# Causal attention inside a fused block: diagonal pieces weighed in float32, probabilities kept in a ring of four where the activations X lay

## What is computed

```python
q, k, v = jnp.split(x @ W_qkv, 3, axis=-1)          # 16 heads of 64
q, k = (apply_rope(q), apply_rope(k))
dots = jnp.einsum('bhid,bhjd->bhij', q, k) * scale
dots = jnp.where(causal, neg, dots)
attn = jax.nn.softmax(dots, axis=-1)
out = jnp.einsum('bhij,bhjd->bhid', attn, v)
out = jax.nn.relu(out @ W_o1) @ W_o2                # then layer norm, times gamma
```

## Time and profile before

| | us |
|---|---|
| median of three runs | 5071.18 |
| the profiled execution, its time | 5068.41 |
| the profiled execution, its span | 5066.7 |
| PE busy | 3697.3 (73%) |
| DVE busy | 3704.5 (73%) |
| ACT busy | 2570.4 (51%) |
| POOL busy | 2389.1 (47%) |
| float16 weighing, three lines | 464.4 + 462.7 + 463.2 |
| the 16 turns of attention, from and to | about 2712 to 4565 |

### The profile page before, as it was taken

How to read it: one execution, slowest core, us unless ns; L and a number is a source line. 1 busy time by engine, 2 the same in 40 slices (tenths; PEclk the granted TensorE clock), 3 DMA queues, 4 the chain that set the end, 5 groups by cost and what they waited for, 6 DMA issues and landing times. The chain is left out here.

```text
span 5066.7 us, 84689 instructions
## 1 busy us (share of the span) xinstructions
PE 3697.3 (73%) x28907; PEld 2605.5 (51%) x28907; DVE 3704.5 (73%) x4463; ACT 2570.4 (51%) x4134; POOL 2389.1 (47%) x1532
## 2 busy tenths in 40 slices
PE   2997645555555569948936998999989898994595
PEld 1663224444434446637813665666656565663484
DVE  6993579999999989930067888888888888885101
ACT  1222456666666632222214676777767676784221
POOL 0220268888888832220034666656656666600202
PEclk9998767777777789959958999999999999996697
DMA  2000001001101000024532222222222222202254
GB/s 86 0 0 4 7 21 32 30 29 30 31 29 29 30 28 0 0 96 153 162 118 55 55 54 48 47 49 68 52 64 53 52 53 54 52 10 91 73 181 155
DMA packets 236314, 276.23 MB, mean 55 GB/s; under 512 B 63820, under 2 KB 183557, under 8 KB 234561
## 3 DMA queue, kind: packets, MB, share of 16 engines
q1 hardware_dynamic: 223056, 244.85, 17.8%
q0 software_dynamic: 8704, 24.35, 1.4%
q10 hardware_dynamic: 4224, 2.76, 0.2%
HBM read 152.60 MB, written 36.04 MB: 37 GB/s over the span
## 5 line engine op out<-in xcount | busy, mean ns | idle before, releaser
L2247 DVE TENSOR_TENSOR att_b_prob_low<-att_b_prob,att_b_prob_high 128x1024 f16<-128x1024 f32 (+2 forms) x640 | 780.4, 1220 | 64.0 <-ACT att_b_prob_high L2214 55.2
L2274 DVE TENSOR_REDUCE att_b_neg_max<-att_b_peek 128x1 f32<-128x1024 f32 (+1 forms) x748 | 667.8, 906 | 143.1 <-PE att_b_peek L2102 115.8
L2212 ACT ACTIVATE att_b_prob<-att_b_score,att_soft 128x1024 f32<-128x1024 f32 (+2 forms) x640 | 633.7, 990 | 219.9 <-PE att_b_score L2125 145.7
L1030 PE MATMUL mix_scan_hT<-ident,mix_scan_h 128*128 128x128 f32 x1024 | 248.7, 389 | 536.1 <-DVE mix_scan_h L978 502.1
L2214 ACT ACTIVATE att_b_prob_high<-att_b_score,att_soft 128x1024 f16<-128x1024 f32 (+2 forms) x640 | 630.8, 986 | 10.1 <-PE att_b_o L2153 3.6
L1030 PEld LDWEIGHTS mix_scan_hT<-ident,mix_scan_h 128*128 128x128 f32 x1024 | 172.5, 197 | 650.7 <-DVE mix_scan_h L978 443.9
L2149 PE MATMUL att_b_o<-att_b_vh,att_b_prob_high 128*128 128x65 f16 x4352 | 464.4, 195 | 36.9 <-DVE att_b_prob_low L2247 27.5
L2123 PE MATMUL att_b_score<-att_b_q_both,att_b_k_twice 128*128 128x512 f16 (+3 forms) x1280 | 450.5, 352 | 31.4 <-ACT att_b_prob_high L2214 21.9
L2149 PEld LDWEIGHTS att_b_o<-att_b_vh,att_b_prob_high 128*128 128x128 f16 x4352 | 402.4, 98 | 128.8 <-DVE att_b_prob_low L2247 73.5
L2153 PE MATMUL att_b_o<-att_b_vh,att_b_prob_low 128*128 128x65 f16 x4352 | 463.2, 194 | 0.0
L2151 PE MATMUL att_b_o<-att_b_vl,att_b_prob_high 128*128 128x64 f16 x4352 | 462.7, 193 | 0.0
(11 more groups left out here) (344 smaller groups left out, 9612.7 us busy)
## 6 DMA issues: line engine op xcount, KB each, us to landing
moe_w<-in_L_ffn_W_dram SPq DMA_DIRECT2D x64, 1024.0 KB, 8.1
mix_scan_b_row<-mix_b_rows SPq DMA_DIRECT2D x128, 256.0 KB, 3.2
att_b_crossed<-att_b_raw SPq DMA_DIRECT2D x512, 64.0 KB, 2.0
att_b_q_both<-att_b_halves SPq DMA_DIRECT2D x240, 64.0 KB, 2.0
att_b_k_twice<-att_b_halves SPq DMA_DIRECT2D x240, 64.0 KB, 2.0
moe_slots_in<-moe_route_zero SPq DMA_DIRECT2D x2, 4096.0 KB, 14.6
moe_exp_x<-moe_slots_in SPq DMA_DIRECT2D x32, 256.0 KB, 4.5
moe_slots_out<-moe_exp_y POOLq DMA_DIRECT2D x32, 256.0 KB, 6.5
```

The source lines that it names most:

```text
L1030: last = pe.transpose(hT_ps[:, j * D + m * P:j * D + (m + 1) * P], hs[:, b * W + m * GRP + t * P:b * W + m * GRP + (t + 1) * P], ident[:, :])
L2212: act.activation(prob[:, at:at + width], score[m % 2][:, 0:width], ACT.Exp, scale=soft[:, 0:1])
L2247: dve.tensor_tensor(prob_low[:, at:at + width], prob[:, at:at + width], prob_high[:, at:at + width], ALU.subtract).then_inc(low_ready, 1)
L2274: last = dve.tensor_reduce(neg_max[:, first + col:first + col + 1], peek_bank(kind, s)[:, base:base + nb * P], AX.X, ALU.max, negate=True)
```

## The change

Pieces with the diagonal (WHOLE) are no longer split. ACT writes their exponential once, to float32; DVE does nothing for them; PE weighs each block with one float32 matmul of the float32 probabilities and a float32 copy of V (`v_whole`, 65 columns with its column of ones). For this ACT copies each of V's four jobs twice, to float32 and to float16, the float32 copy first. The other pieces are weighed as before.

`prob` now holds four pieces, and together with `headsT` lies in the first 5120 columns of X. These columns (128 x 5120 float32, 2.5 MB) are stored to `lent` in DRAM when the stage begins, ahead of the tables, and fetched back at the start of the first `attention_out`, behind the fetch of the first sequence's sums; DVE waits for both fetches before it adds to X. ACT waits for the store before the first exponential. The float32 exponential of piece m now waits for the last reader of piece m - 4, which is PE for a diagonal piece and DVE for another. `low_ready` counts split pieces only (`split`).

```diff
+WHOLE = [PIECES_S[n][1][0][0] >= PIECES_S[n][0] * GT for n in range(NH)]
+SPLITS = [m for m in range(STEPS) if not WHOLE[m % NH]]
...
+PROBS = 4
+BORROWED = PROBS * SPAN + 2 * GRP
...
+        v = sb("v", [P, 2 * QT * 2 * COL])
+        v_whole = v[:, :].rearrange("p (s e) -> p s e", e=COL)
-        prob = sb("prob", [P, 2 * SPAN])
+        prob, headsT = X[:, 0:PROBS * SPAN], X[:, PROBS * SPAN:BORROWED]
...
                     load_weights(0, 0)
+                    sp.dma_start(lent, X[:, 0:BORROWED]).then_inc(x_lent, 16)
                     sp.dma_start(cos[:, :], rope[0]).then_inc(tables, 16)
                     sp.dma_start(sin[:, :], rope[1]).then_inc(tables, 16)
...
+            pool.memset(v_whole[:, :, ONE:ONE + 1], 1.0).then_inc(masks, 1)
...
-                pe.wait_ge(low_ready, piece(t, m + 1))
+                if WHOLE[n]:
+                    pe.wait_ge(expd, piece(t, m + 1))
+                else:
+                    pe.wait_ge(low_ready, split(t, m + 1))
...
+                    if WHOLE[n]:
+                        last = pe.matmul(out, prob[:, whole], v_whole[:, s, 0:HEAD + 1], start=first, stop=final,
+                                         skip_group_check=True)
+                        continue
...
+                if kind == FIRST:
+                    act.wait_ge(x_lent, 16)
...
+                    act.copy(v_whole[:, at:at + GT * 2, 0:HEAD], side_ps[:, :].rearrange("p (s d) -> p s d", d=HEAD))
                     act.copy(v_cols[:, at:at + GT * 2, 0:HEAD], side_ps[:, :].rearrange("p (s d) -> p s d", d=HEAD))\
                         .then_inc(v_high, 1)
...
             def exponents(t, m):
-                at, width = m % 2 * SPAN, width_of(m)
+                to, at, width = m % PROBS * SPAN, m % 2 * SPAN, width_of(m)
                 act.wait_ge(scored, piece(t, m + 1))
-                wait_unless_first(act, low_ready, piece(t, m - 1))
-                act.activation(prob[:, at:at + width], score[m % 2][:, 0:width], ACT.Exp, scale=soft[:, 0:1])
+                if WHOLE[(m - PROBS) % NH]:
+                    wait_unless_first(act, p_done, piece(t, m - PROBS + 1))
+                else:
+                    wait_unless_first(act, low_ready, split(t, m - PROBS + 1))
+                ins = act.activation(prob[:, to:to + width], score[m % 2][:, 0:width], ACT.Exp, scale=soft[:, 0:1])
+                if WHOLE[m % NH]:
+                    ins.then_inc(expd, 1)
+                    return
...
-                    if has_piece(kind, v - 1):
+                    if has_piece(kind, v - 1) and not WHOLE[(v - 1) % NH]:
                         low_part(t, v - 1)
...
-            if fetch:
-                sp.dma_start(fetch[0][:, :], fetch[1]).then_inc(fetch[2], 16)
+            for to, parked in fetch:
+                sp.dma_start(to, parked).then_inc(fetched, 16)
...
             steps = QT // GT
+            dve.wait_ge(fetched, 2 * 16)
```

More of the change, by code:

```diff
@@ L1520, in experts_and_attention, with attention_outputs @@
             acc = inner.enter_context(nc.sbuf_tensor(f"{name}_acc", [P, QT * D], F32))
-            attention_heads(nc, ident, dram, rope, xh, xl, unit, per_unit, soft, acc, x_parked, acc_parked, name + "_b")
-            attention_outputs(nc, X, ident, dram, acc, acc_parked, name)
-def attention_outputs(nc, X, ident, dram, acc, acc_parked, name):
+            lent = nc.dram_tensor(f"{name}_lent", (P, BORROWED), F32, kind="Internal").ap()
+            attention_heads(nc, X, ident, dram, rope, xh, xl, unit, per_unit, soft, acc, x_parked, acc_parked, lent,
+                            name + "_b")
+            attention_outputs(nc, X, ident, dram, acc, acc_parked, lent, name)
+def attention_outputs(nc, X, ident, dram, acc, acc_parked, lent, name):
     with ExitStack() as ctx:
@@ L1529, in attention_outputs @@
         fetched = nc.alloc_semaphore(name=f"{name}_fetched")
-        attention_out(nc, X, ident, dram, acc, 1, f"{name}_out1", (earlier, acc_parked, fetched))
-        attention_out(nc, X, ident, dram, earlier, 0, f"{name}_out0", None, fetched)
+        attention_out(nc, X, ident, dram, acc, 1, f"{name}_out1", ((earlier[:, :], acc_parked), (X[:, 0:BORROWED], lent)), fetched)
+        attention_out(nc, X, ident, dram, earlier, 0, f"{name}_out0", (), fetched)
 def combine_for_attention(nc, X, ident, dram, xh, xl, unit, per_unit, soft, x_parked, wide, weight, get, slots_out, name):
@@ L1826, in attention_heads @@
         inv = sb("inv", [P, GT])
-        heads, headsT = sb("heads", [P, QT * PAIR]), sb("headsT", [P, 2 * GRP])
+        heads = sb("heads", [P, QT * PAIR])
         score = [ps("score0", SPAN), ps("score1", SPAN)]
@@ L1850, in attention_heads, with split @@
         piece = lambda t, m: t * STEPS + m
+        def split(t, m):
+            return t * len(SPLITS) + sum(1 for u in SPLITS if u < m) - sum(1 for u in SPLITS if u >= m + STEPS)
         slot = lambda p, s: p * STEPS + s
@@ L2144, in weigh @@
                 for k, at, i in blocks:
+                    whole = slice(m % PROBS * SPAN + at, m % PROBS * SPAN + at + P)
                     at = slice(m % 2 * SPAN + at, m % 2 * SPAN + at + P)
@@ L2246, in low_part @@
                 wait_unless_first(dve, p_done, piece(t, m - 1))
-                dve.tensor_tensor(prob_low[:, at:at + width], prob[:, at:at + width], prob_high[:, at:at + width],
+                dve.tensor_tensor(prob_low[:, at:at + width], prob[:, fro:fro + width], prob_high[:, at:at + width],
                                   ALU.subtract).then_inc(low_ready, 1)
@@ L2313, in _, with attention_out @@
             dve.wait_ge(added, out_count(STREAM, 0))
-def attention_out(nc, X, ident, dram, acc, batch, name, fetch=None, fetched=None):
+def attention_out(nc, X, ident, dram, acc, batch, name, fetch, fetched):
     T0 = batch * QT
@@ L2340, in _ @@
                 .then_inc(w_loaded, 16)
-            if fetch:
-                sp.dma_start(fetch[0][:, :], fetch[1]).then_inc(fetch[2], 16)
+            for to, parked in fetch:
+                sp.dma_start(to, parked).then_inc(fetched, 16)
         @block.scalar
         def _(act):
-            if fetched is not None:
-                act.wait_ge(fetched, 16)
+            if not fetch:
+                act.wait_ge(fetched, 2 * 16)
             def first(t, b):
```

12 lines of the change are left out of this document (6 added, 6 removed).

## The result

The changed kernel takes 5085.6 us (median of 6 runs, 5075.4 to 5091.9), the kernel before 5073.8 on the same chip (6 runs, 5064.5 to 5079.4): ratio 1.0024, 95% interval 1.0014 to 1.0034. It is **slower by 12 us**, where 5035 and a gain were forecast. The profiled execution took 5085.0 us, with a span of 5083.4.

The account below looks back on a forecast made before the run. POOL's chain was taken to bound steps 0 to 22 of a turn, PE and DVE alternately steps 22 to 39. -2.5 us over 15 turns (-37.5) plus +3 at the start, on 5068.4, gave 5034, forecast as 5035 us, range 4980 to 5105.

Parts of the forecast that it names:

- A float32 block costs 0.222: PE's weighing: two records of 0.111 us a block, 0.132 more than before; eighty blocks a turn add 10.6 us.
- rival (c): PE's float32 weighing: load and matmul in series, 0.153 us a record, +5.5 us a turn, 5154 us; chance 0.09.
- POOL's chain loses 3.9 us, the first part 3.5 and 0.5 for the clock: Steps 0 to 22: fewer subtractions shorten POOL's six jobs by 3.9; 0.4 given back for PE; -0.5 for a shorter stall.
- Second part: PE +23 blocks, 3.0 us, where it has 44.3 of work in 48.7 ... I take +1.5: Steps 22 to 39: PE's dearer weighing partly fits in its room; net +1.5 us a turn, ends -1 and +5.
- DVE's relief in the second part: Steps 22 to 39: DVE's 6 us less help only where DVE leads; included in the +1.5 a turn.
- The extra V copies: ACT's float32 copy of V delays PE's next V job by up to 0.59 us, four times a turn.
- ACT's relief costs or gives nothing: Each turn: ACT's 10.4 us net saving is worth nothing by itself, as ACT mostly waits for PE or POOL.
- Start +3 (0 to 12): Before attention: X's store ahead of the tables delays them some 8 to 10 us, just reaching DVE's first rotation; +3 us.
- X's way back: nothing: First attention_out: X is back near 4589, wanted at 4600.8, so no cost; without that cover up to 12 us.
- The last turn: nothing: Last turn, led by ACT: its pairs lose 1.6 us there and gain 1.3 on PE; net nothing.
- rival (b): Each turn: gains and losses cancel, 1.5 in the first part, 1.3 back in the second; 5068 us; chance 0.15.
- rival (a): Steps 22 to 39 and heavy first-part pairs: PE becomes the bound, +3.5 us a turn, 5124 us; chance 0.15.

Follow-up runs that it names:

- e4: Changed kernel, diagonal pieces weighed in float32, but ACT still writes their high part and DVE still subtracts, into unread buffers; ratio 1.0106 to the kernel before.
- e9: Changed kernel with float32 weighing only for head 1's diagonal pieces (steps 20 to 39), head 0 weighed as before; ratio 1.0068 to the kernel before.
- e3: Changed kernel, diagonal pieces without float32 exponential or subtraction, weighed by three float16 matmuls, the third reading the high part; ratio 0.9920 to the kernel before.
- e8: Kernel before, with DVE's instruction in diagonal pieces reading scores from PSUM instead of float32 probabilities from SBUF; PE's scores wait for it; ratio 0.9967.
- e1: Changed kernel with only the ring of four and X's store and fetch kept, all pieces weighed as before, no float32 V; 5062.5 us against 5059.9, ratio 1.0006.
- e11: Changed kernel with float32 weighing only for head 0's three diagonal pieces of 7 blocks (4, 10, 18); ratio 0.9919 to the kernel before.
- e6: Changed kernel with float32 weighing only for six diagonal pieces of head 0 (4, 5, 10, 11, 18, 19); ratio 0.9936 to the kernel before.
- e2: Changed kernel with float32 weighing only for head 0's diagonal pieces (steps 0 to 19), head 1 weighed as before; 5032.4 us, ratio 0.9940 to the kernel before.

## Why the prediction was wrong

The two effects were named rightly: a shorter chain of POOL, and dearer weighing on PE. The step that failed is the room for PE's price in the second part. Point by point:

- *A float32 block costs 0.222*: 0.223 in the row above. The Trainium skill's rule that was weighed ("TensorE: Matmul & The Clock Gate", Part 3, The mechanism), no overlap of load and matmul in one row group, would by the prediction's own estimate have given 0.153 a record. 0.111 was measured, as at 16 columns, so the trace disagrees with it here too and rival (c) is out.
- *POOL's chain loses 3.9 us, the first part 3.5 and 0.5 for the clock*: the chain lost 2.3 (53.2 to 50.9), the first part 3.1. The wait for `k_low` fell from 47.0 to 15.4 us, and the granted clock of the first part rose from 0.95 to 0.98 in the mean of 15 turns. Right in kind, 0.9 us too much a turn. POOL's own work in the six jobs did fall by 3.7 us (50.5 to 46.8), and the 1.5 us that PE now makes it wait are what is missing. That 3.7 comes near 3.9 is partly luck: 8 diagonal subtractions lie beside the six jobs and not 10, and they cost POOL 2.9 us and not 35% of the whole. The other subtractions cost it 1.0 less after the change, because they meet it elsewhere; in e4 POOL's work falls by 1.7 with every subtraction in place.
- ***"Second part: PE +23 blocks, 3.0 us, where it has 44.3 of work in 48.7 ... I take +1.5"* is the step that failed.** The part grew by 3.1 in the mean of all turns (49.7 to 52.8), and by as much in e4 and e9: the price was paid in full. The 44.3 came from counting columns. The windows view of the very part shows PE busy for 47.21 of 48.41 us at a granted clock of 0.98, which is 46.3 us of work, so there were 2.1 us of room at most where the sum had 4.4 and set half of the price against them, and nothing of it was used. The same count gave 52.6 for the first part, where the row says 57.80; there most of the difference is the clock, since 57.80 at 0.93 is 53.8 of work. PE's own row had been read (102 of 118) and then replaced by the count of 96.9.
- *DVE's relief in the second part*: hardly anything (e3, 0.3 us). *The extra V copies*: some 0.3 us of the 3.1, by PE's wait for V's low part. *ACT's relief costs or gives nothing*: e8 bears it out, with the whole gain of the first part and ACT's work as before.
- *Start +3 (0 to 12)*: +1.2 and +2.5 in the two profiles, and e1 as a whole is at 1.0006. *X's way back: nothing*: right, the fetch is issued at 4584.61 and lands 15.3 us later, and X is added to at 4617.81. *The last turn: nothing*: not refuted. The stretch behind POOL's last rotation took 147.0 us before and 151.0 and 151.5 after, 147.6 with head 0 alone. It also holds the second part of the turn before the last, which is 3.1 us longer, so some 1 us is left for the last turn, less than the edges scatter.

With 3.1 for the second part and 3.1 for the first, a turn is at zero instead of at -2.5: 1.6 us of the miss lie in the second part and 0.9 in the first, over 15 turns 24 and 14 us. The edges add 6 or 7: 5068.4 + 6 to 7 = 5075, against 5085.0 in the first profile, 5073.5 without its 11.5 us. The total is near rival (b), gains and losses that cancel, which had 0.15. Its sizes were other ones: (b) had 1.5 in the first part and 1.3 back. The second part went as in rival (a), with all 23 blocks exposed (3.1 of the 5 us that (a) put on it), and the first part gained twice what both rivals left it.

The fastest kernel with a full result is e11, with e6 and e2 near it (their intervals overlap): float32 only for large pieces weighed beside POOL's chain, 5020.2 us against 5061.9, 0.8% under the kernel before and faster than the changed one.

## What to carry to other kernels

A change that trades one engine's work for another's is worth something only stage by stage: give it to the steps in which the relieved engine is waited for and the paying one has room, and leave the rest as it was (0.9940 for the one half, 1.0068 for the other, 1.0024 for both). Whether the paying engine has room is read from its busy row in just that stretch; where a count of columns comes out lower than the row, take out what the granted clock explains, and for the rest trust the row. A gap that a row shows in one place (PE's 5.6 us before step 22) is no room anywhere else.

## What was not expected of the hardware

- A DVE subtraction with both operands in SBUF and a POOL operation slow each other, and the one that began second pays: 325 POOL operations that begin during a subtraction are 0.66 us longer, 65 small subtractions that begin during a POOL operation 0.57. Taking one of DVE's operands from PSUM was worth as much to POOL (chain 53.2 to 50.3) as leaving the subtraction out (51.1).
- So what a subtraction costs POOL isn't proportional to its length: 2.5 us less of subtraction in small pieces moved the chain by 0.4 us, 3.8 us less in large ones by 2.5.
- One profile held 11.5 us more in one stage than the 12 others, the same program's second one among them (61.9 against 50.4 us).
